# Four graph layers on one core: where the tables are turned, and who makes the distances in the sort

## The chip, the cores and the metric

The kernel runs on one core of a Trainium2 chip. The metric is the device time of one execution in microseconds, the median of several runs. The core has five engines with instruction streams of their own: TensorE (PE, with its weight loads as PEld), VectorE (DVE), ScalarE (ACT), GpSimd (POOL) and SyncE (SP, which here only issues transfers and waits). Transfers go through 16 DMA engines. Engines wait for one another with semaphores.

## The reference

There are 6250 nodes of 128 features and 200000 edges (src, dst), each with a type of 2, a type of 64 and a weight. Four graph layers follow one another, each as `x = layernorm(x + layer(x))`:

```python
x = _layernorm(x + _L0_gnn_ref(x, edge_index, edge_type_64, ...), axis=-1)      # mean of (x[src] + rel[type]) @ W_msg.T
x = _layernorm(x + _L1_gnn_ref(x, src, dst, edge_weight, ...), axis=-1)         # 4 heads, softmax over the edges of a source, norm per head
x = _layernorm(x + _L2_gnn_ref(x, edge_index, edge_type_2, ...), axis=-1)       # sum over edges, weights by type, relu
x = _layernorm(x + _L3_gnn_ref(x, edge_index, L3_gnn_W, L3_gnn_b), axis=-1)     # degree-normed sum over edges in the other direction
```

## The kernel before

The nodes are laid out in 49 tiles of 128 (NT = 49). The edges are first sorted into the 49 x 49 pairs of tiles. For each pair a one-hot product on TensorE gives a 128 x 128 table of edge counts, and every layer multiplies tables by node features. The program runs in stages, each a block that starts only when all engines have left the one before.

The sort (lines 300 to 830) works on 226 units in two phases: 49 of level 1, then 177 of levels 2 and 3 in turn. A unit holds 32 columns (level 1) or 28 (levels 2 and 3) of 128 records. For unit n, VectorE makes one-hot digits (`hot`), TensorE counts them (`count`, some 9 to 16 matmuls), ScalarE takes the counts out of PSUM (`looked`), VectorE sums them to `rank` (`ranks`), and ScalarE writes the ranks twice side by side as `place` (`paired`). Then a permutation matrix `PM` is needed for each column: 1 where the place equals the index. VectorE makes most columns by comparison with `iota_b` (`equal`). The last SHARE columns (6, 5, 4 for levels 1, 2, 3) are ScalarE's: `distances` (line 474) squares `rank - index`, one ACTIVATE with a bias for each column, and `near` (line 484) turns the squares into 1 or 0 with Relu(1 - square). TensorE's `route` (line 628) moves the records with one matmul per column, 32 or 28 of them, and waits for both VectorE's and ScalarE's columns. ScalarE takes the result out (`evict`). Order on TensorE in iteration n: `count(n+2)`, then now and then the linear part of the first layer (lines 651 to 658), then `route(n)`. Order on ScalarE: `paired(n)`, `distances(n)`, `evict(n-1)`, copies of the linear part, `double(n+3)`, `near(n)`, `looked(n+2)`.

The first layer (`aggregate_relation_turned`) makes 343 groups of seven tables each ([128, 7 x 128] in bf16, 224 KB), and SP stores each to DRAM as `tab_d` (line 1188). The second layer (`aggregate_weighted`, block at line 1612) makes its own weighted tables on TensorE, ScalarE and VectorE and moves nothing: its SP program loads one vector and is then done. The third layer (`aggregate_typed_turned`) reads the stored groups back with plain transfers (line 1931) into a ring of five buffers. The fourth (`aggregate_plain_turned`) needs each table turned. Its SP issues for each of the 343 units one `dma_start_transpose` (line 2336) that gathers seven tables from DRAM and writes them turned into a ring of five buffers (`kept`, in `sl_f`). A buffer is issued again once the conversion that read it is done. Conversion from bf16 to fp32r (line 2322) goes to `tables_r`, two buffers: even units on VectorE, odd units on ScalarE, and a conversion waits for the matmuls of the unit two before. TensorE then does four matmuls (line 2454). After each 49 units the sums are taken out by ScalarE (`sumT`, line 2428), turned by TensorE (line 2464), and seven tiles of nodes are normed by VectorE and ScalarE in slots between the units.

## Time and profile before

| | us |
|---|---|
| median of 3 runs | 4126.3 (4124.19 to 4128.95) |
| profiled execution | 4132.2, its span 4130.5 |
| TensorE busy | 3511.6 (85%) |
| VectorE busy | 3204.4 (78%) |
| ScalarE busy | 2337.2 (57%) |
| mean granted TensorE clock | 0.963 |
| chain that ended last | 10% DMA `sl_f<-tables`, in the fourth layer |

The span falls into the sort (from the start to about 1000 us), the first layer (to about 1788), the second (1788.7 to 2815.9), the third (to 3641) and the fourth (3645 to the end). A share of busy time over the whole span says little: each stage has a limit of its own, and a block ends when its last engine is done. The views used below are the windows (busy time by engine in a stretch), the lines of one instruction (durations, times to landing), the waits and the timeline.

### The profile page before, as it was taken

To read this page: it belongs to the slowest core of one execution; us is meant where nothing else is said; L and a number is where in the kernel's file an instruction comes from. 1 tells how busy PE (TensorE), PEld (TensorE's weight loads), DVE (VectorE), ACT (ScalarE), POOL (GpSimd) and SP (SyncE) were. 2 spreads that over 40 slices of the span, in tenths; PEclk is the share of its full clock that TensorE was granted. 3 is DMA by queue.
4 is the path that set the end of the run, shared out by engine and by line. 5 is a ranking of instruction groups with operands and counts; after the bars stand their busy time and mean duration, and the time that the engine had idled before them with its cause. 6 is when DMAs were issued, how large, how long until landed. Compare 5 with 4: busy or idle time off the path is not lost. (4 is left out here: it accounts for less than half of the span.)

```text
span 4130.5 us, 90438 instructions
## 1 busy us (share of the span) xinstructions
PE 3511.6 (85%) x36615; PEld 2901.3 (70%) x36740; DVE 3204.4 (78%) x3960; ACT 2337.2 (57%) x5142; POOL 391.8 (9%) x336
## 2 busy tenths in 40 slices
PE   2666777776999999869999999996999999967776
PEld 1555666664666666569999999995888888845554
DVE  7999999998777777589999999996666666723233
ACT  4998999996555555423333333334666666634343
POOL 3003211122111111100000000001000000000000
PEclk9999999997999999879999999998999999989999
DMA  3000000001322222200000000002333333268988
GB/s 107 2 2 2 2 2 2 2 2 37 114 110 110 111 111 110 77 2 2 2 2 2 2 2 2 2 2 85 99 101 101 99 101 103 86 116 170 168 170 172
DMA packets 423099, 257.10 MB, mean 62 GB/s; under 512 B 329994, under 2 KB 419863, under 8 KB 422548
## 3 DMA queue, kind: packets, MB, share of 16 engines
q1 hardware_dynamic: 422196, 248.79, 22.7%
q8 instruction: 299, 4.90, 0.5%
q10 hardware_dynamic: 480, 2.40, 0.2%
q14 instruction: 124, 1.02, 0.1%
HBM read 86.93 MB, written 85.49 MB: 42 GB/s over the span
## 5 line engine op out<-in xcount | busy, mean ns | idle before, releaser
L97 DVE TENSOR_TENSOR both_hot<-iota_own,recs 128x1792 bf16<-128x1792 bf16 (+1 forms) x686 | 754.4, 1107 | 231.5 <-PE rR L1466 121.9
L1830 ACT ACTIVATE gC<-qC 128x896 f32<-128x896 f32 x343 | 314.7, 918 | 647.6 <-PE qC L1850 647.6
L1862 PE MATMUL qO<-A,gC 128*128 128x132 f32 x4802 | 615.3, 280 | 0.0
L1862 PEld LDWEIGHTS qO<-A,gC 128*128 128x128 f32 x4802 | 566.6, 190 | 0.0
L1474 PE MATMUL rO<-sl_f,terms 128*128 128x384 bf16 (+1 forms) x1934 | 476.4, 355 | 3.7 <-DVE A L1242 2.2
L2174 ACT ACTIVATE some_r<-rC 128x512 fp32r<-128x512 f32 (+1 forms) x686 | 336.4, 543 | 252.6 <-PE rC L2204 252.1
L628 PE MATMUL pV<-VO,PM 128*128 128x70 bf16 (+4 forms) x6524 | 259.8, 199 | 236.2 <-ACT PM L484 159.7
L1432 ACT ACTIVATE sl_f<-rC 128x896 bf16<-128x896 f32 x343 | 313.8, 915 | 255.2 <-PE rC L1454 254.4
L2454 PE MATMUL tO<-tables_r,Xr 128*128 128x448 f32 x1372 | 357.6, 392 | 116.5 <-ACT tables_r L2322 80.1
L91 DVE TENSOR_TENSOR PM<-iota_b,place 128x2944 bf16<-128x2944 bf16 (+2 forms) x226 | 410.4, 1816 | 30.8 <-ACT place L464 30.4
L1466 PE MATMUL rR<-rel_hot,both_hot 128*128 128x65 bf16 x2450 | 410.9, 194 | 25.5 <-DVE A L1242 12.2
L628 PEld LDWEIGHTS pV<-VO,PM 128*128 128x128 bf16 x6524 | 238.6, 100 | 260.2 <-issue 258.3
L2454 PEld LDWEIGHTS tO<-tables_r,Xr 128*128 128x128 f32 x1372 | 234.7, 190 | 237.0 <-ACT tables_r L2322 145.1
L2322 DVE CAST tables_r<-sl_f 128x896 fp32r<-128x896 bf16 x172 | 107.8, 627 | 331.6 <-DMA sl_f<-tables 312.0
L1668 DVE TENSOR_TENSOR g<-sl_f 128x2688 bf16<-128x2688 bf16 (+1 forms) x229 | 363.9, 1589 | 0.2 <-PE qC L1850 0.2
L2216 PE MATMUL rK<-some_r,Xr 128*128 128x512 f32 (+1 forms) x1372 | 363.4, 386 | 0.0
L1850 PE MATMUL qC<-g,sl_f 128*128 128x128 bf16 x4908 | 313.9, 220 | 49.0 <-DVE g L1668 48.7
L2216 PE MATMUL rA<-all_r,Xr 128*128 128x512 f32 (+1 forms) x1372 | 342.0, 371 | 1.9 <-DVE all_r L1975 1.9
L474 ACT ACTIVATE apart_b<-iota_b,rank 128x128 bf16<-128x128 bf16 x1093 | 342.6, 396 | 0.0
L1474 PEld LDWEIGHTS rO<-sl_f,terms 128*128 128x128 bf16 x2058 | 202.1, 98 | 194.3 <-issue 20.3
L1850 PEld LDWEIGHTS qC<-g,sl_f 128*128 128x128 bf16 x4908 | 292.4, 98 | 58.1 <-DVE g L1668 54.7
L2322 ACT ACTIVATE tables_r<-sl_f 128x896 fp32r<-128x896 bf16 x171 | 162.6, 951 | 283.2 <-DMA sl_f<-tables 263.7
(298 smaller groups left out, 6225.4 us busy)
## 6 DMA issues: line engine op xcount, KB each, us to landing
tables<-sl_f SPq DMA_DIRECT2D x343, 224.0 KB, 1.9
sl_f<-tables SPq DMA_DIRECT2D x343, 224.0 KB, 2.5
sl_f<-tables SPq DMA_TRANSPOSE x343, 3.7
edges<-terms SPq DMA_DIRECT2D x1, 3528.0 KB, 11.2
B<-in_x SPq DMA_DIRECT2D x1, 2744.0 KB
out<-B SPq DMA_DIRECT2D x7, 392.0 KB
terms<-in_edge_type ACTq DMA_DIRECT2D x2, 686.0 KB
terms<-in_edge_weight ACTq DMA_DIRECT2D x1, 686.0 KB
```

The costliest lines, as they stand in the source:

```text
L91: return v.tensor_tensor(o.rearrange("p n (a b) -> p n a b", b=2), (iota_own if own else iota_b)[:, at:at + w].rearrange("p (a b) -> p a b ...
L97: return v.tensor_tensor(o.rearrange("p n k (a b) -> p (n k) a b", b=2), iota_own[:, 0:w].rearrange("p (a b) -> p a b", b=2).unsqueeze(1). ...
L474: ins = act.activation(apart_b[:, j, :], iota_b[:, 0:P], ACT.Square, scale=-1.0, bias=rank[:, n % 2, col:col + 1])
L628: mm = pe.matmul(pV[n % 2][:, g * row:(g + 1) * row].rearrange("p (f b) -> p f b", f=u.nf), PM[:, n % 2, col, :], values[:, :, col, :], st ...
L1466: return pe.matmul(pR[:, to:to + DW], both_hot[:, U % HOTS, j, 0, :], rel_hot[:, K % 2, a % FOUR * n + j, 0:DW], start=a == 0 and j == 0, ...
L1474: mm = pe.matmul(pO[:, h, 0:(hi - lo) * P], X[:, a, s, :], of_half(kept[U % RING], h), start=a == 0 and s == 0, stop=a == NT - 1 and s == ...
L1668: v.tensor_tensor(h1[:, U % 2, 0:n, :, :].rearrange("p n s (a b) -> p n s a b", b=2), bare[U % 3][:, 0:n, 1, :].rearrange("p n (a b) -> p ...
L1850: mm = pe.matmul(pC[U % 2][:, tile_in_group(q, j), :], bare[U % 3][:, j, 0, :], h1[:, U % 2, j, s, :], start=s == 0 and (q > 0 or j != 1), ...
L1862: mm = pe.matmul(pO[i % SUMS][:, 0:XW], Cs[:, U % 2, j, :], A[:, a, :], start=a == 0, stop=a == NT - 1)
L2174: act.activation(of_half(some_r[:, U % 2, :], h).rearrange("p (n d) -> p n d", d=P), pC[Q % 3][:, 0:hi - lo, :], ACT.Copy).then_inc(s_cs, 1)
L2216: mm = pe.matmul((pA if whole else pK)[:, h, 0:(hi - lo) * P], Xr[:, a, s * P:(s + 1) * P], of_half((all_r if whole else some_r)[:, U % 2, ...
L2454: mm = pe.matmul(pO[:, h, 0:HW], Xr[:, b, s * P:(s + 1) * P], table_h[:, h, :], start=b == 0 and s == 0, stop=b == NT - 1 and s == 1, skip ...
```

## The change

Two edits that don't touch each other.

First, the turned tables. A second DRAM tensor `turned_d` is added, and a buffer of three slots in SBUF. In the second layer, SP now issues for each unit a transposing transfer from `tab_d` into a slot, waits for it two units later, and stores the slot to `turned_d`. Before a slot is used again its store must have landed. The fourth layer then reads `turned_d` with plain transfers. The waits of the third and fourth layers on `s_tab` count the additional transfers.

Second, the sort. The distances `place - index` are made by TensorE: for groups of four columns, one matmul with an identity over the broadcast places and one with minus the identity over the index, summed in PSUM (`pZ`). ScalarE squares all of them with one ACTIVATE. SHARE for level 3 goes from 4 to 5. `looked(n+1)` now stands behind `paired(n)`, and `distances(n)` behind `evict(n-1)`. On TensorE `apart_from(n)` stands at the head of iteration n, between `route(n-1)` and `count(n+2)`. GpSimd makes two more constants, and VectorE and TensorE wait for 14 constants where they waited for 12.

```diff
-            SHARE = (6, 5, 4)
+            SHARE = (6, 5, 5)
...
+                    gp.tensor_scalar(whole_b[:, :], ident_f[:, :], 1.0, None, ALU.mult).then_inc(consts, 1)
+                    gp.tensor_scalar(minus_b[:, :], ident_f[:, :], -1.0, None, ALU.mult).then_inc(consts, 1)
+                    gp.wait_ge(consts, 14)
...
+                        act.wait_ge(s_far, n + 1)
                         if n >= 1:
                             act.wait_ge(s_rest_perm, n)
-                        for j in range(share):
-                            col = cols - share + j
-                            ins = act.activation(apart_b[:, j, :], iota_b[:, 0:P], ACT.Square, scale=-1.0, bias=rank[:, n % 2, col:col + 1])
-                        ins.then_inc(s_pair, 1)
+                        act.activation(apart_b[:, 0:share, :], pZ[:, 0:share, :], ACT.Square).then_inc(s_pair, 1)
...
                             paired(n)
-                            distances(n)
+                            if n > a and n + 1 < b:
+                                looked(n + 1)
                             if n > a:
                                 evict(n - 1)
+                            distances(n)
...
                             near(n)
-                            if n + 2 < b:
-                                looked(n + 2)
...
+                    def apart_from(n):
+
+                        u = units[n]
+                        cols, share = u.npos * u.ngrp, SHARE[u.level - 1]
+                        pe.wait_ge(s_pair, 2 * n + 1)
+                        for a in range(0, share, 4):
+                            w = min(4, share - a)
+                            held = place[:, n % 2, cols - share + a:cols - share + a + w, 0:1].broadcast_to([P, w, P])
+                            pe.matmul(pZ[:, a:a + w, :], whole_b[:, :], held, start=True, stop=False, skip_group_check=True)
+                            mm = pe.matmul(pZ[:, a:a + w, :], minus_b[:, :], iota_b[:, 0:P].unsqueeze(1).broadcast_to([P, w, P]), start=False, stop=True, skip_group_check=True)
+                        mm.then_inc(s_far, 1)
...
                         for n in range(a, b):
+                            apart_from(n)
                             if n + 2 < b:
                                 count(n + 2)
```

```diff
+        TURNS = 3
+        TURNED = [STORED[b] + (32 * len(range(b, UNITS, TURNS)) if b < TURNS else 0) for b in range(RING)]
...
+                        for U in range(UNITS + TURNS - 1):
+                            if U < UNITS:
+                                m, b = U // NT, U % NT
+                                first = b // G7 * NT + m * G7
+                                if U >= TURNS:
+                                    sp.wait_ge(s_tab[U % TURNS], STORED[U % TURNS] + 32 * (U // TURNS))
+                                sp.dma_start_transpose(turning[:, U % TURNS, :], tab_d[first:first + G7, :, b % G7 * P:(b % G7 + 1) * P].rearrange("u p d -> (u p) d")).then_inc(s_tab[U % TURNS], 16)
+                            done = U - (TURNS - 1)
+                            if done >= 0:
+                                sp.wait_ge(s_tab[done % TURNS], STORED[done % TURNS] + 32 * (done // TURNS) + 16)
+                                sp.dma_start(turned_d[done], turning[:, done % TURNS, :]).then_inc(s_tab[done % TURNS], 16)
+                        for b in range(TURNS):
+                            sp.wait_ge(s_tab[b], TURNED[b])
...
-                            m, b = unit(U)
-                            first = b // G7 * NT + m * G7
-                            table = tab_d[first:first + G7, :, b % G7 * P:(b % G7 + 1) * P].rearrange("u p d -> (u p) d")
-                            sp.dma_start_transpose(kept[U % RING], table).then_inc(s_tab[U % RING], 16)
+                            sp.dma_start(kept[U % RING], turned_d[U]).then_inc(s_tab[U % RING], 16)
```

## Rows read from the trace of the kernel before

**Rows 1.** Windows: second, third, fourth layer; length, PE, PEld, DVE, ACT, POOL, clock, DMA share.

```profile
1788.70:2815.90 1027.20, 980.26 (x12152) 966.80 (x12152) 991.37 (x950) 356.68 (x429) 96.19 (x99) 0.99 0.01 2
2815.90:3641.00 825.10, 798.49 (x5716) 665.00 (x5716) 557.52 (x805) 532.38 (x998) 0.00 (x0) 0.98 0.33 97
3645.07:4114.90 469.83, 360.64 (x1413) 239.85 (x1414) 139.57 (x286) 184.92 (x225) 0.00 (x0) 0.99 0.90 169
```

**Rows 2.** Waits of SP: us in total, times, longest; the second layer's block end.

```profile
SPq L1612 <- PEq L1612: 1027.2, 1, 1027.2
```

**Rows 3.** Line 2336, transposing transfers: ns to issue; first one alone, then all.

```profile
L2336 SPq DMA_TRANSPOSE sl_f<-tables x1: 1261/1261/1261, 3645.1 to 3645.1; - x1
...
DMA to landing us min/median/max: 3.5/3.5/3.5
...
L2336 SPq DMA_TRANSPOSE sl_f<-tables x343: 1150/1287/2780, 3645.1 to 4110.1; - x172
```

**Rows 4.** Line 1188, plain stores of the first layer: ns to issue, us to landing.

```profile
L1188 SPq DMA_DIRECT2D tables<-sl_f x343: 332/332/357, 1005.9 to 1717.6; - x172
...
DMA to landing us min/median/max: 1.9/1.9/4.5
```

**Rows 5.** Windows behind the first transposing issue: last columns clock, DMA share, GB/s.

```profile
3646.25:3646.50 0.25, 0.00 (x0) 0.00 (x0) 0.00 (x0) 0.00 (x0) 0.00 (x0) 0.50 0.11 27
...
3647.50:3647.75 0.25, 0.00 (x0) 0.00 (x0) 0.00 (x0) 0.00 (x0) 0.00 (x0) 0.50 0.50 103
```

**Rows 6.** A plain store's issue (timeline) and its last window of traffic.

```profile
1301.14 0.33 SPq L1188 DMA_DIRECT2D tables<-sl_f  x1
...
1302.50:1302.75 0.25, 0.25 (x6) 0.13 (x3) 0.00 (x0) 0.25 (x2) 0.00 (x0) 1.00 0.26 86
```

**Rows 7.** Timeline of the fourth layer where buffers were full: start, length, what.

```profile
3721.88 0.95 ACT L2322 ACTIVATE tables_r<-sl_f 128x896 fp32r<-128x896 bf16 x1 [2.19 <-PE tO L2454]
...
3724.06 0.95 ACT L2322 ACTIVATE tables_r<-sl_f 128x896 fp32r<-128x896 bf16 x1 [1.23 <-PE tO L2454]
```

**Rows 8.** Waits in the fourth layer: TensorE for the sums being taken out.

```profile
PE tO L2454 <- ACT sumT L2428: 7.7, 6, 1.6
```

**Rows 9.** Line 723, the ranks, one for each unit of the sort.

```profile
L723 DVE TENSOR_REDUCE rank<-M x226: 259/558/695, 67.7 to 979.0; 128x28 f32<-128x392 bf16 x47, 128x28 f32<-128x448 bf16 x37, 128x32 f32<-128x448 bf16 x25, 128x28 f32<-128x112 bf16 x4
```

**Rows 10.** Timeline of the sort, level 1: near, route, count, double, the next route.

```profile
181.72 0.92 ACT L484 ACTIVATE PM<-apart_b,ones_f 128x768 bf16<-128x768 bf16 x1
...
182.89 1.44 PE L628 MATMUL pV<-VO,PM 128*128 128x84 bf16 x32 [1.61 <-ACT PM L484]
...
184.17 0.35 PE L607 MATMUL pR<-O,tri_b 128*128 128x448 bf16 x1
...
185.35 0.56 ACT L435 ACTIVATE V<-terms 128x448 bf16<-128x448 bf16 x1
...
186.99 1.44 PE L628 MATMUL pV<-VO,PM 128*128 128x84 bf16 x32 [1.61 <-ACT PM L484]
```

**Rows 11.** Timeline of the sort, level 2: two routes in a row.

```profile
280.18 1.08 PE L628 MATMUL pV<-VO,PM 128*128 128x70 bf16 x28 [1.96 <-ACT PM L484]
...
283.57 1.08 PE L628 MATMUL pV<-VO,PM 128*128 128x70 bf16 x28 [0.87 <-ACT PM L484]
```

**Rows 12.** Groups: ScalarE's distances; then ScalarE reading PSUM, 312 and 896 elements.

```profile
L474 ACT ACTIVATE apart_b<-iota_b,rank 128x128 bf16<-128x128 bf16 x1093 | 342.6, 396 | 0.0
...
L493 ACT ACTIVATE terms<-pV 128x312 bf16<-128x312 f32 x38 | 16.1, 423 | 2.7 <-PE pV L628 2.7
...
L1432 ACT ACTIVATE sl_f<-rC 128x896 bf16<-128x896 f32 x343 | 313.8, 915 | 255.2 <-PE rC L1454 254.4
```

**Rows 13.** Groups by shape, 315 to 975 us: VectorE's comparisons, 24 and 23 columns.

```profile
L91 DVE TENSOR_TENSOR PM<-iota_b,place 128x3072 bf16<-128x3072 bf16 x85 | 153.0, 1801 | 8.7 <-ACT place L464 8.7
L91 DVE TENSOR_TENSOR PM<-iota_b,place 128x2944 bf16<-128x2944 bf16 x83 | 144.2, 1737 | 19.4 <-ACT place L464 19.1
```

**Rows 14.** Timeline at the sort's start: GpSimd's last constant, which VectorE waits for.

```profile
63.47 0.55 POOL L373 TENSOR_SCALAR lift<-ident_f 128x128 bf16<-128x128 f32 x1
```

More of the change, by code:

```diff
@@ L68, in gnn_four_layers_kernel @@
     tab_d = nc.dram_tensor("tables", (UNITS, P, G7 * P), BF16, kind="Internal").ap()
+    turned_d = nc.dram_tensor("turned_tables", (UNITS, P, G7 * P), BF16, kind="Internal").ap()
     with ExitStack() as ctx:
@@ L170, in gnn_four_layers_kernel @@
             lift = sb("lift", [P, P], BF16, c1)
+            whole_b = sb("whole_b", [P, P], BF16, c1)
+            minus_b = sb("minus_b", [P, P], BF16, c1)
             drop = sb("drop", [P, 1], F32, c1)
@@ L198, in gnn_four_layers_kernel @@
             pV = [ps(f"pV{i}", [P, 512], c1) for i in range(2)]
-            pD = ps("pD", [P, 512], c1)
+            pZ = ps("pZ", [P, 8, P], c1)
             pL = ps("pL", [P, 2, P], c1)
             pW = ps("pW", [P, 512], c1)
+            pD = pW
             names = ("loads", "pads", "consts", "tri_made", "prep", "fields", "blanks", "packed", "s_pad0", "s_load0", "s_xin0", "s_stored", "turned", "wt_made",
-                     "s_dup", "s_hot", "s_cnt", "s_look", "s_taken0", "s_more", "s_pair", "s_val", "s_perm", "s_rest_perm", "s_out", "s_ev",
+                     "s_dup", "s_hot", "s_cnt", "s_look", "s_taken0", "s_more", "s_pair", "s_val", "s_perm", "s_rest_perm", "s_far", "s_out", "s_ev",
                      "s_tp0", "s_xt0", "s_y0", "s_own0", "s_high0", "s_rest0", "s_mid0", "s_low0", "s_wt0", "s_total", "s_words", "s_named", "s_kind", "s_left", "s_last")
             (loads, pads, consts, tri_made, prep, fields, blanks, packed, s_pad, s_load, s_xin, s_stored, turned, wt_made,
-             s_dup, s_hot, s_cnt, s_look, s_taken, s_more, s_pair, s_val, s_perm, s_rest_perm, s_out, s_ev,
+             s_dup, s_hot, s_cnt, s_look, s_taken, s_more, s_pair, s_val, s_perm, s_rest_perm, s_far, s_out, s_ev,
              s_tp, s_xt, s_y, s_own, s_high, s_rest, s_mid, s_low, s_wt, s_total, s_words, s_named, s_kind, s_left, s_last) = [sem(n, c1) for n in names]
@@ L373, in _ @@
                     gp.tensor_scalar(lift[:, :], ident_f[:, :], LIFT, None, ALU.mult).then_inc(consts, 1)
-                    gp.wait_ge(consts, 12)
+                    gp.tensor_scalar(whole_b[:, :], ident_f[:, :], 1.0, None, ALU.mult).then_inc(consts, 1)
+                    gp.tensor_scalar(minus_b[:, :], ident_f[:, :], -1.0, None, ALU.mult).then_inc(consts, 1)
+                    gp.wait_ge(consts, 14)
                     def low_parts(m):
@@ L630, in route @@
                         mm.then_inc(s_out, 1)
-                    pe.wait_ge(consts, 12)
+                    pe.wait_ge(consts, 14)
                     for a, b in phases:
@@ L702, in _ @@
                     v.wait_ge(prep, PREP)
-                    v.wait_ge(consts, 12)
+                    v.wait_ge(consts, 14)
                     def hot(n):
@@ L1592, in aggregate_weighted @@
                 Cs = sb("gC1", [P, 2, G7, P], F32, c)
+                turning = sb("turning1", [P, TURNS, G7 * P], BF16, c)
                 vec = sb("vec1", [P, P], F32, c)
@@ L1973, in convert @@
                                 v.wait_ge(s_all, U - 1)
-                            v.wait_ge(s_tab[U % RING], STORED[U % RING] + 16 * (U // RING + 1))
+                            v.wait_ge(s_tab[U % RING], TURNED[U % RING] + 16 * (U // RING + 1))
                             v.tensor_copy(all_r[:, U % 2, :], kept[U % RING]).then_inc(s_kept[0], 1)
@@ L2119, in convert @@
                                 act.wait_ge(s_all, U - 1)
-                            act.wait_ge(s_tab[U % RING], STORED[U % RING] + 16 * (U // RING + 1))
+                            act.wait_ge(s_tab[U % RING], TURNED[U % RING] + 16 * (U // RING + 1))
                             act.activation(all_r[:, U % 2, :], kept[U % RING], ACT.Copy).then_inc(s_kept[1], 1)
@@ L2312, in fetched @@
                 def fetched(U):
-                    return 2 * STORED[U % RING] + 16 * (U // RING + 1)
+                    return TURNED[U % RING] + STORED[U % RING] + 16 * (U // RING + 1)
                 def converted(eng, U):
```

## The prediction

> **What bounds the kernel now.** I read the windows by stage first, then who waits inside each stage the change touches, then the timeline there. In the second layer TensorE is busy 980 of 1027 us and VectorE 991, and the DMA engines stand idle at a share of 0.01 [rows 1]. SP has nothing to do there: it waits 1027.2 us for the block to end [rows 2]. In the fourth layer no engine is full (TensorE 361 of 470 us), but the DMA share is 0.90 [rows 1]. Each of its 343 units costs SP a transposing issue of 1.29 us, and the first one, with nothing in flight, already took 1.26 [rows 3]. 343 x (1.29 + 0.03 to the next) is 453 of the 470 us, so the fourth layer goes by SP's issuing. In the sort two engines are level: the level-1 period is 4.10 us from route to route (182.89 to 186.99) [rows 10], which is VectorE's four operations back to back, and ScalarE's list is just as long. The whole span's 57% for ScalarE hides that.
>
> **The fourth layer, where work is removed.** The transposing issue (1.29 us) becomes a plain one (0.33 us for a plain transfer of the same 224 KB) [rows 3, 4]. The ring of five then no longer sets the pace: the third layer drew 97 GB/s at a DMA share of 0.33 [rows 1], so a unit costs 0.33 x 825 / 343 = 0.79 us of the DMA engines. Late next is the pair of buffers `tables_r`: an odd unit's conversion (ScalarE, 0.95 us), its four matmuls, then the next odd conversion. The trace shows this loop bare where the ring was full: conversions start at 3721.88 and 3724.06 [rows 7], 2.18 us for two units, 1.09 for one. 343 x 1.09 = 374. To it comes a first landing of about 3 us, and six changes of tile group, which can no longer hide behind the ring: TensorE waits 7.7 / 6 = 1.3 us for the sums [rows 8], turns seven tiles (I put 0.9), and VectorE's three wide additions overfill its slots (I put 1.7): an estimate of 3.9 us, 24 for six. 374 + 3 + 24 = 401 against 470: minus 69. Bounds: minus 95 if nothing of the 24 shows, minus 55 if it is half as much again.
>
> **The second layer, where SP gets work.** This is the largest term. 343 transposing issues and 343 stores go on SP's queue, in one order. Iteration U is: wait for the store of U-3, issue transpose U, wait for transpose U-2, issue store U-2. But the store of U-3 was issued in iteration U-1, right before. Three slots do not help: every iteration contains a whole store from issue to landing. The wait for transpose U-2 costs nothing, it was issued two iterations earlier.
>
> The room is 1027.2 / 343 = 2.99 us per unit [rows 2]. The need, from below: 1.31 us until the store can be issued (1.29 and the step to it), 1.9 us until it has landed, the shortest and the median of 343 stores alone [rows 3, 4], 0.04 to go on: 3.25 us. From above: the store goes on the same queue right behind a transpose whose data has barely begun. The transpose issued at 3645.07 has its traffic from about 3646.4 (0.11 in that window, its issue just over) to the dip at 3647.6 [rows 5], so 1.3 to 2.6 us after its issue. A store issued at 1301.14 has sent its last bytes at about 1302.6, in a burst of 0.6 to 0.7 us [rows 6], and lands 0.4 us after. Behind the transpose the burst lies at 2.6 to 3.25, and the landing at 3.7: 3.75 with the step. I take 3.6, near the upper end, because the DMA engines are full with the transpose when the store's data would begin at 2.05; I leave something for the ragged start and end of its traffic.
>
> The end: 342 iterations and the last transpose and store one behind the other (3.5 + 1.9). 1788.7 + 342 x 3.6 + 5.4 = 3025, where the block now ends at 2815.9: plus 209. At 3.25 it is plus 90, at 3.75 plus 261. All engines wait for SP there, and the third layer cannot start. That the DMA engines are idle in this layer is true and no cover: a chain of latencies is what has to fit, not a transfer rate.
>
> A rule points the same way. The Trainium skill ("DMA: Bandwidth & Descriptors", section "Queues, rings and completion order") says that a ring is consumed in order and that a semaphore's increment lands only after all earlier writes of that DMA engine. By it a store's landing cannot come before the transpose's own, 3.5 us after its issue, so the lower bound of 3.25 would be 3.55. No row here shows a plain transfer behind a transpose, so I keep 3.25 as a bound.
>
> **The sort.** At the start GpSimd makes two more constants like `lift`, 0.55 us each [rows 14], and VectorE and TensorE wait for them: plus 1. Removed are ScalarE's 6, 5 or 4 activations, 342.6 / 1093 = 0.31 us each; added is one reading PSUM: from 0.42 us for 312 elements and 0.92 for 896, 0.81 for 768 and 0.70 for 640 [rows 12]. ScalarE gains 1 us per unit, yet VectorE is as full as it was in level 1. VectorE gains only 1.80 - 1.74 us for 86 units of level 3 (5 us) and the waits for `place`, 8.7 + 19.1 us [rows 13]: at most minus 33.
>
> Against that, the new wait closes a loop that did not exist: `route(n)`, then on the same queue `apart_from(n+1)`, then ScalarE's square, `double`, `near`, and `route(n+1)`, which needs `near`. Before, ScalarE made its distances while TensorE routed. Queued behind the wait for `s_far` on ScalarE are `double` and `near`; TensorE waits for these. Level 1, from the rows: `near` ends at 182.64 and route starts at 182.89, 0.25; route to the next matmul 1.28 (182.89 to 184.17) [rows 10]; 2 x 768 columns at 2.4 GHz 0.64; tail of the last matmul 0.16 (0.35 less the 0.19 of 448 columns); to ScalarE 0.1; square 0.81 - 0.1; double 0.56 - 0.1; near 0.92 [rows 10, 12] (0.1 is what neighbours on ScalarE overlap). Sum 4.52 against 4.10: 48 periods x 0.42 = plus 20. Level 2: route 1.08 instead of 1.44, 640 columns, the rest a little shorter, some 3.76 against 3.39 (280.18 to 283.57) [rows 11]. But the mean of the second phase is well above 3.39: from 67.7 to 979.0 us there are 225 periods [rows 9], less 48 x 4.10, so 177 of 4.04. Its extra work (the linear part, words, clock at its lower level) may cover the longer loop or add to it. I take plus 0.08 each, plus 15; bounds minus 33 and plus 62 (0.35 each). Sort: plus 36, from minus 12 (1 + 20 - 33) to plus 83; minus 32 if the loop of level 1 is not closed either.
>
> **Sum.** 209 - 69 + 36 = plus 176. The profiled span of 4130.5 would be 4307; the median of the runs lies 4 us below that span, so 4126.3 + 176 = 4302.
>
> **Rivals.** A: the forecast, SP's chain of about 3.6 us; 4302, its own range 4215 to 4390.
>
> B: the store is not held up by the transpose in front, 3.25 us. For it: the stores landed in 1.9 us while anything else was going on. Against: those had an empty queue. 4126 + 90 - 69 + 36 = 4183.
>
> C, the other side: SP's chain fits under TensorE and VectorE, so the second layer keeps its 1027 us. Mechanism: the 1.26 us issue is not SP's own work but the queue pushing back, and in a queue that is drained every iteration it falls to a plain issue's 0.33 [rows 4], so an iteration is 2.3 us. It decides from 3.09 us down, where (1027.2 + 33 - 5.4) / 342 the added end eats the gain. For it: 1.29 is nearly the pace of the fourth layer. Against: the very first issue, nothing in front, took 1.26 [rows 3]. 4126 - 69 + 36 = 4093, or 4025 if the sort gives its 33 as well. The Trainium skill ("Advanced Engine Details and Errata", section "X-Bar Transpose (TRN2)") says that transposing transfers are as fast as regular ones, which would be this rival; the trace has 169 GB/s in the fourth layer [rows 1] against some 350 in a plain store's burst (224 KB in 0.65 us [rows 6]), so I don't follow it.
>
> D: reading `tab_d` and writing `turned_d` at once makes both slower, 4.2 us: plus 415, 4508.
>
> That the edit in the sort does not relieve ScalarE is not a rival: five activations of 0.31 become one of 0.7. Whether that relief reaches the end is the question above.
>
> **Chances.** A 0.62, B 0.17, C 0.12, D 0.09. The range 4125 to 4420 takes in A and B and leaves out most of C, D. About 0.2% (8 us) is what a measurement of this kernel can tell from no change. Faster: most of C and a thin end of B with the sort's best case, 0.12. Same: 0.03. Slower: 0.85.
>
> **What would show it.** In the changed kernel, SP's wait for the end of the block in the second layer is gone and the others wait for SP, some 200 us; DMA there shows a period of 3.6 us, with stores landing in about 2.3 instead of 1.9. The fourth layer's conversions wait for matmuls, 2.18 us apart, and DMA leaves the chain that ended last. In the sort, TensorE's idle time before `route` is given to `near`, and level 1 runs at 4.5 us per unit. I am wrong if the second layer still ends with TensorE's last matmul, or if the level-1 period stays at 4.10.

## The result, and the profile after

The changed kernel takes 4363.06 us (median, 4361.89 to 4379.83) against 4127.62 for the kernel before on the same chip: a ratio of 1.0582 (1.0561 to 1.0602), 235 us slower. The profiled execution has a span of 4360.2 us against 4130.5, so 229.7 us have to be found. SP's waits in the second layer (us in total, times, longest):

```profile
SPq L1642 <- DMA turned_tables<-turning: 693.9, 340, 4.1
SPq L1646 <- DMA turning<-tables: 0.9, 1, 0.9
```

In place of the one wait of 1027.2 us for the others [rows 2] SP now waits 340 times for a store to land, and only once for a transpose. The ends of the block, line 1632, say who was late:

```profile
L1632 PEldq DRAIN  x1: 2188/2188/2188, 2797.3 to 2797.3; - x1
...
L1632 DVEq DRAIN  x1: 911/911/911, 2821.6 to 2821.6; - x1
...
L1632 SPq COMPARE_BRANCH  x1: 41/41/41, 3126.6 to 3126.6; - x1
```

The other engines are done at 2822.5, 1027.9 us after the layer began at 1794.6, which is their old time. SP follows 304 us later. Its issues there (ns to issue, shortest/median/longest, first and last; below each line the us from issue to landing):

```profile
L1642 SPq DMA_TRANSPOSE turning<-tables x343: 1151/1152/2172, 1795.0 to 3121.5; - x172
...
DMA to landing us min/median/max: 2.9/3.1/5.1
...
L1646 SPq DMA_DIRECT2D turned_tables<-turning x343: 320/578/1044, 1799.1 to 3124.7; - x172
...
DMA to landing us min/median/max: 1.9/2.4/4.7
```

(3121.5 - 1795.0) / 342 is 3.88 us for one iteration. But it is not the same all along. The timeline of SP in the tail, where all others stand, and windows beside one another (columns as in [rows 1]):

```profile
2999.09 1.15 SPq L1642 DMA_TRANSPOSE turning<-tables  x1
3000.29 0.58 SPq L1646 DMA_DIRECT2D turned_tables<-turning  x1
3002.68 1.15 SPq L1642 DMA_TRANSPOSE turning<-tables  x1
```

```profile
1900.00:2000.00 100.00, 96.69 (x1194) 94.82 (x1192) 97.11 (x101) 32.55 (x37) 7.25 (x10) 1.00 0.46 114
2850.00:2950.00 100.00, 0.00 (x0) 0.00 (x0) 0.00 (x0) 0.00 (x0) 0.00 (x0) 0.50 0.48 125
```

In the tail an iteration takes 3.59 here and 3.61 on average (83 iterations from 2821.8 to 3121.5); while the engines run, 259 issues in 1026.8 us make 3.96. The traffic says the same: 114 against 125 GB/s.

The fourth layer, in the timeline at its end and over all (the matmuls of line 2484):

```profile
4099.95 0.95 ACT L2355 ACTIVATE tables_r<-sl_f 128x896 fp32r<-128x896 bf16 x1 [1.24 <-PE tO L2484]
4100.96 1.88 PE L2484 MATMUL tO<-tables_r,Xr 128*128 128x448 f32 x8 [0.28 <-ACT tables_r L2355]
4102.13 0.95 ACT L2355 ACTIVATE tables_r<-sl_f 128x896 fp32r<-128x896 bf16 x1 [1.23 <-PE tO L2484]
```

```profile
L2484 PE MATMUL tO<-tables_r,Xr x1372: 358/367/742, 3959.4 to 4344.8; 128*128 128x448 f32 x196
```

ScalarE's conversions stand 2.18 us apart. Of the 343 conversions 311 wait for matmuls now, where it was 21 before: the loop over the two buffers sets the pace all along, and not only where the ring happened to be full [rows 7]. From the first transfer's issue, 3956.2, to the last matmul, 4344.8, it is 388.6 us against 469.8: minus 81. Of the chain that ended last, transfers are 0% now where they were 10%.

The sort, level 1 in the timeline, then all ranks:

```profile
179.30 0.81 ACT L479 ACTIVATE apart_b<-pZ 128x768 bf16<-128x768 f32 x1 [0.22 <-PE pZ L628]
180.47 0.93 ACT L488 ACTIVATE PM<-apart_b,ones_f 128x768 bf16<-128x768 bf16 x1
181.66 1.45 PE L644 MATMUL pV<-VO,PM 128*128 128x84 bf16 x32 [1.34 <-ACT PM L488]
182.94 0.38 PE L627 MATMUL pZ<-place,whole_b 128*128 128x512 bf16 x1
183.14 0.43 ACT L497 ACTIVATE terms<-pV 128x312 bf16<-128x312 f32 x1 [1.07 <-PE pV L644]
183.79 0.81 ACT L479 ACTIVATE apart_b<-pZ 128x768 bf16<-128x768 f32 x1 [0.22 <-PE pZ L628]
```

```profile
L740 DVE TENSOR_REDUCE rank<-M x226: 258/558/619, 68.7 to 992.5; 128x28 f32<-128x392 bf16 x47, 128x28 f32<-128x448 bf16 x37, 128x32 f32<-128x448 bf16 x25, 128x28 f32<-128x112 bf16 x4
```

Square to square is 4.49 us (and 4.53 in some periods), against 4.10 [rows 10], and TensorE waits for `PM`, ScalarE for `pZ` and `pV`, in a closed ring. The last rank comes at 992.5 instead of 979.0 [rows 9].

The ledger: up to the last rank +13.5; from there to the second layer -7.6 (802.1 instead of 809.7); the second layer +305.1 (1332.3 instead of 1027.2); from its end to the fourth's first issue +0.1; the fourth layer -81.2; behind it -0.2. Together 229.7.

### The profile page after: what moved, and what is told of

Read it like the earlier page. It is cut to its first block and busy times, and to the rows that moved or that the text cites. A ratio compares the mean times of both kernels' runs of the same rounds, so it can differ in the third digit from the quotient of the medians.

```text
span 4360.2 us, 92418 instructions
## 1 busy us (share of the span) xinstructions
PE 3580.6 (82%) x37643; PEld 2962.3 (68%) x37644; DVE 3207.1 (74%) x3960; ACT 2206.9 (51%) x4275; POOL 389.8 (9%) x338
## 5 line engine op out<-in xcount | busy, mean ns | idle before, releaser
L1493 PE MATMUL rO<-sl_f,terms 128*128 128x512 bf16 (+1 forms) x2058 | 500.3, 354 | 19.7 <-DVE A L1261 13.0
L2237 PE MATMUL rC<-both_hot 128*128 128x128 bf16 x2450 | 197.3, 221 | 336.3 <-DVE both_hot L98 336.3
L92 DVE TENSOR_TENSOR PM<-iota_b,place 128x2944 bf16<-128x2944 bf16 (+1 forms) x226 | 407.4, 1803 | 14.3 <-ACT place L470 13.9
L2237 PEld LDWEIGHTS rC<-both_hot 128*128 128x128 bf16 x2450 | 138.4, 98 | 392.5 <-DVE both_hot L98 341.5
L2008 DVE CAST all_r<-sl_f 128x896 fp32r<-128x896 bf16 x172 | 107.6, 626 | 397.9 <-DMA sl_f<-tables 311.4
L2484 PE MATMUL tO<-tables_r,Xr 128*128 128x448 f32 x1372 | 329.4, 382 | 64.0 <-ACT tables_r L2355 42.5
L2484 PEld LDWEIGHTS tO<-tables_r,Xr 128*128 128x128 f32 x1372 | 245.3, 189 | 145.9 <-ACT tables_r L2355 104.6
```

Source lines behind the costliest of these rows:

```text
L92: return v.tensor_tensor(o.rearrange("p n (a b) -> p n a b", b=2), (iota_own if own else iota_b)[:, at:at + w].rearrange("p (a b) -> p a b ...
L1493: mm = pe.matmul(pO[:, h, 0:(hi - lo) * P], X[:, a, s, :], of_half(kept[U % RING], h), start=a == 0 and s == 0, stop=a == NT - 1 and s == ...
L2237: mm = pe.matmul(pC[Q % 3][:, to - lo, :], both_hot[:, U % HOTS, j, 1, :], both_hot[:, U % HOTS, j, 0, :], start=m > 0 or j != 1, stop=m > ...
L2484: mm = pe.matmul(pO[:, h, 0:HW], Xr[:, b, s * P:(s + 1) * P], table_h[:, h, :], start=b == 0 and s == 0, stop=b == NT - 1 and s == 1, skip ...
```

## The experiments

**Is it the turned tables, and those alone?** The change in halves: `e3_turn_only` has the sort of the kernel before, `e4_sort_only` the second to fourth layers of the kernel before.

> The kernel before with the edit of the tables alone, the sort as before. Theory: all of the loss is here: plus 305 in the second layer, minus 81 in the fourth, about 4351, some 14 us under the changed kernel. Rival (the new sort costs nothing of its own, its 14 us are the clock's): 4363.

> The kernel before with the edit of the sort alone. Theory: level 1 is 0.42 us per unit longer (plus 20), the second phase a little shorter (minus 8), plus 1 for the constants: plus 13 in the sort, 4127 + 13 = 4140, less what the first layer gains in clock (8 us in the profile of the changed kernel). Rival (ScalarE's relief shows): below 4120.

Measured: the tables alone 4352.11 (4347.4 to 4355.6), ratio 1.0546 (1.053 to 1.0562); the sort alone 4142.42 (4141.12 to 4147.87), ratio 1.004 (1.0026 to 1.0054). Neither half is a gain, and the two add up: 223 + 14 against 235.

**Is it that the store stands behind the transpose on the queue?** `e1_store_first` issues in each iteration the same two transfers in the other order, the store of U-2 ahead of transpose U. `e2_four_slots` leaves the order and gives the store one slot more, so that the one waited for was issued an iteration earlier.

```diff
                        for U in range(UNITS + TURNS - 1):
+                            done = U - (TURNS - 1)
+                            if done >= 0:
+                                sp.wait_ge(s_tab[done % TURNS], ...)
+                                sp.dma_start(turned_d[done], turning[:, done % TURNS, :])...
                             if U < UNITS:
                                 ...
                                 sp.dma_start_transpose(turning[:, U % TURNS, :], ...)...
-                            done = U - (TURNS - 1)
-                            if done >= 0:
-                                ...
```

```diff
-        TURNS = 3
+        TURNS = 4
-                        for U in range(UNITS + TURNS - 1):
+                        for U in range(UNITS + TURNS - 2):
-                            done = U - (TURNS - 1)
+                            done = U - (TURNS - 2)
```

> The changed kernel with one edit on SP in the second layer: in each iteration the store of unit U-2 is issued before the transposing transfer of unit U, not behind it. The same 686 transfers, the same three slots. Theory (the period is a chain: issue of the transpose, then a whole store from issue to landing, because the store waited for was issued in the iteration just before): the landing now runs under the next transpose's issue, the period falls from 3.9 us to about 2 us, 343 x 2 = 690 us fits under the 1027 us of TensorE and VectorE, and the second layer ends at its old length. Time 4363 - 305 = about 4058. Rival (the DMA engines or the mix of reading and writing DRAM set the 3.9 us, whatever the order): the period stays above 3.5 us and the time above 4300.

> The changed kernel with four slots instead of three, and the store still two units behind the transpose and issued after it: the store waited for is now one iteration older. Theory of the chain: two iterations hold one transpose issue, one store landing and another transpose issue, so the period falls to 2 to 2.4 us and the second layer is back at about 1027 us, the time at about 4060. If only the order on the queue mattered (a store behind a transpose is slow), the period would stay above 3.5 us.

Measured: 4062.5 (4057.04 to 4067.5), ratio 0.9841 (0.9826 to 0.9856); and 4066.7 in a single run. The same two transfers in another order are worth 300 us. SP is now done before the others (ns to issue, landing, then the layer's windows):

```profile
L1646 SPq DMA_TRANSPOSE turning<-tables x343: 1149/1200/2773, 1799.9 to 2599.4; - x172
...
DMA to landing us min/median/max: 3.0/3.2/5.8
```

```profile
2000.00:2200.00 200.00, 196.70 (x2449) 194.32 (x2449) 195.00 (x184) 73.61 (x91) 18.15 (x20) 1.00 0.92 197
```

An iteration is (2599.4 - 1799.9) / 342 = 2.34 us, far less than 3.61, and under the 2.99 that the layer allows. The DMA engines are at 0.92 with 197 GB/s while TensorE is busy 196.70 of 200 us, as it was with next to no traffic beside it (196.69 in the same window of the kernel before, at a share of 0.01): in this layer the transfers don't slow the computing. The second layer was lost to latencies in a row, not to a rate.

**Is it the transposing transfer, or any transfer in front of the store?** `e5_plain_in` replaces the transpose by a plain load of the same size; it leaves out the turning, and reads one stored group where the transpose gathers seven tables.

```diff
-                                sp.dma_start_transpose(turning[:, U % TURNS, :], tab_d[...])...
+                                sp.dma_start(turning[:, U % TURNS, :], tab_d[U])...
```

> The changed kernel with the transposing transfer of the second layer replaced by a plain load of the same 224 KB (the tables stay unturned, so the fourth layer sums over the wrong side); order, slots and waits as in the changed kernel. Theory of the chain: an iteration is the issue of the load (0.33 us) and a whole store, 0.33 + 2.4 + 0.1 = 2.8 to 3.2 us with the disturbances of the busy part, so the second layer is near or little over its 1027 us, the time 4060 to 4110. Rival (the traffic of reading and writing at once sets the 3.9 us): it stays above 4300.

Measured: 4186.89 in a single run, 77 us over the upper end of what was expected. An iteration is (2950.3 - 1804.2) / 342 = 3.35 us, although the issue in front of the store is short:

```profile
L1642 SPq DMA_DIRECT2D turning<-tables x343: 319/320/431, 1804.2 to 2950.3; - x172
...
DMA to landing us min/median/max: 2.4/2.7/4.3
...
L1646 SPq DMA_DIRECT2D turned_tables<-turning x343: 319/432/1671, 1808.2 to 2953.0; - x172
...
DMA to landing us min/median/max: 1.9/2.9/4.6
```

The store, issued 0.4 us behind the load, lands 2.9 us after its issue, where one with nothing in front lands in 1.9 [rows 4]. Both kernels say the same: the store lands 0.5 to 0.6 us after the transfer ahead of it has landed. Plain: 0.4 + 2.9 = 3.3 against 2.7. Transposing, in the quiet tail: issued 1.2 after the transpose and landing in 2.4 is 3.6, against 3.1. That is the forecast's upper picture, and it doesn't need the transpose. The Trainium skill ("DMA: Bandwidth & Descriptors", section "Queues, rings and completion order") has a ring consumed in order and the increment after earlier writes; these traces agree, with 0.5 to 0.6 us on top. They don't separate the order of the queue from the 16 DMA engines that both transfers share: no run issues the store from another queue.

**Why 3.96 us while the engines run, and 3.61 when they stand?** In the timeline some iterations are 1 to 2 us longer. One of them, with the windows of traffic in it (last columns DMA share and GB/s):

```profile
1806.71 0.58 SPq L1646 DMA_DIRECT2D turned_tables<-turning  x1
1811.18 1.15 SPq L1642 DMA_TRANSPOSE turning<-tables  x1
```

```profile
1808.50:1809.00 0.50, 0.50 (x10) 0.48 (x9) 0.50 (x1) 0.00 (x0) 0.00 (x0) 1.00 0.00 0
1809.00:1809.50 0.50, 0.50 (x12) 0.50 (x10) 0.50 (x1) 0.00 (x0) 0.00 (x0) 1.00 0.05 5
1809.50:1810.00 0.50, 0.50 (x11) 0.50 (x8) 0.31 (x1) 0.01 (x1) 0.00 (x0) 1.00 0.07 11
1810.00:1810.50 0.50, 0.50 (x6) 0.50 (x6) 0.44 (x1) 0.50 (x1) 0.00 (x0) 1.00 0.81 307
```

For 1.5 us next to nothing moves; then the rest comes. The view of the DMA queues has, beside the queue of the data, two that bring instructions. First from 1795 to 2822 us, then in the tail (packets, MB, share of 16 engines):

```profile
q8 instruction: 96, 1.57, 0.7%
q14 instruction: 25, 0.20, 0.1%
```

```profile
q14 instruction: 1, 0.01, 0.0%
```

Counted by iteration between 1800 and 2820 us, a packet belonging to the iteration in which it begins: the 146 in which neither queue has a packet take 3.62 us on average, and none is over 4.2. (The text put on record before the next run has 154 of them, with the same average, and 3.57 for the tail.) The 96 with a packet of q8 take 4.53, and 54 of them are over 4.2; the 13 with one of q14 alone take 4.02. The 3.62 is the tail's 3.61: TensorE and VectorE at work beside the transfers cost them nothing that shows. In `e1_store_first` it is 2.05 for the 248 without and 3.27 for the 76 with one of q8. To tell the fetching from the mere activity of the engines, `e12_tail_work` puts useless work into the quiet tail: first many small matmuls (many instructions, little data), then wide operations on VectorE and ScalarE (few instructions, much data in SBUF and PSUM).

```diff
+                        pe.wait_ge(s_cs, UN)
+                        for r in range(2000):
+                            mm = pe.matmul(pC[0][:, 0, 0:32], bare[0][:, 0, 0, :], h1[:, 0, 0, 0, 0:32], start=True, stop=True, skip_group_check=True)
+                        mm.then_inc(s_c, 1)
...
+                        act.wait_ge(s_c, UN + 1)
+                        for r in range(130):
+                            act.activation(Cs[:, 0, :, :], pC[0][:, 0:G7, :], ACT.Copy).then_inc(s_cs, 1)
+                            act.wait_ge(s_cs, UN + r + 1)
...
+                        v.wait_ge(s_c, UN + 1)
+                        for r in range(80):
+                            v.tensor_tensor(h1[:, 0, 0:n, :, :]..., ALU.mult).then_inc(s_hot, 1)
+                            v.wait_ge(s_hot, UN + r + 1)
```

> The changed kernel with useless work put behind the second layer's real work, while SP goes on turning tables alone. First 2000 small matmuls on TensorE (4000 instructions with their weight loads, 32 columns, in some 126 us), then, when they are done, 80 wide multiplications on VectorE (some 1.55 us each) and 130 copies out of PSUM on ScalarE (0.92 us), 210 instructions in about 125 us. Open is why SP's iteration takes 3.96 us while the engines run and 3.57 when they stand. In the changed kernel's trace, between 1800 and 2820 us, 154 iterations without any packet of the two instruction queues take 3.62 us on average and none over 4.2; 96 with a packet of the larger instruction queue take 4.53. Theory (the fetching of instructions holds the transfers up): a packet brings some 256 instructions, so the stretch of small matmuls has about 16 packets, each costs 0.9 us, and its iterations take about 4.0 us on average (16 x 0.9 / 34 = 0.42 over 3.57); the stretch of wide operations stays at 3.6. Rival (SBUF and PSUM traffic of busy engines holds the transfers up): the stretch of wide operations has 3.9 and more, that of small matmuls 3.6 to 3.7. If the fetching theory holds, the kernel takes 4363 + 14 = 4377, else 4363 + 15 or more if the wide operations cost their 0.4 on 33 iterations, so only the stretches tell them apart. A window of traffic in a long iteration should show an instruction packet where the transfers stand still.

Measured: the matmuls kept TensorE busy for 52 us, not 126 (26 ns each). SP's transposes in that stretch, 2799 to 2852 us, and its packets; then the stretch of wide operations, 2856 to 2976:

```profile
L1642 SPq DMA_TRANSPOSE turning<-tables x13: 1151/1236/2196, 2800.2 to 2848.6; - x13
```

```profile
q8 instruction: 15, 0.25, 1.9%
```

```profile
L1642 SPq DMA_TRANSPOSE turning<-tables x33: 1151/1152/1659, 2855.8 to 2972.5; - x33
```

```profile
q8 instruction: 1, 0.02, 0.0%
```

From 2800.17 to the issue at 2852.16 it is 13 iterations of 4.00 us; those from 2823.90, with TensorE alone at work, began with 5.51, 4.35 and 4.04. From 2860.04 to 2972.49 it is 31 of 3.63; the quiet rest is 3.60. TensorE itself, too, stops for 0.1 to 0.7 us after every 128 weight loads and 128 matmuls, and 4000 instructions over 15 packets are about as many for each packet (timeline):

```profile
2818.25 3.27 PEld L1916 LDWEIGHTS qC<-g,sl_f 128*128 128x128 bf16 x128 [0.48 <-issue]
...
2822.00 3.27 PEld L1916 LDWEIGHTS qC<-g,sl_f 128*128 128x128 bf16 x128 [0.48 <-issue]
```

So wide operations cost 0.03 and the stretch with the packets 0.40: of the two rivals the fetching stands. That it isn't TensorE's own work follows from the 146 iterations above and from four here, at 2837.8 to 2848.6, which took 3.59 like any other. The size was off: 15 packets on 13 iterations cost 5.2 us, 0.35 each and not 0.9. The time of 4359.26 us, a single run, is 18 under the 4377 expected; at this size it tells nothing.

Those four iterations have a packet each, so a packet alone doesn't decide. What a packet costs depends on when it begins, counted from the iteration's transposing issue. In the changed kernel the 23 iterations with a packet in the first 1.3 us take 4.11 us on average. The 38 in which it begins 2.25 to 3.0 us in, while both transfers are under way, take 5.27, and none is under 4.84; the long one shown above is of these, with its packet at 2.76. The 19 in which it begins 3.1 to 3.5 us in, when the transpose has just landed, take 3.72, with one at 5.24 and all others at most 3.89. `e3_turn_only` has 5.24 for 39 and 3.80 for 29 in the same two groups. The four of `e12_tail_work` lie at 3.07 to 3.25. By what path a packet stops the other transfers is open.

**Is the pair of buffers what is late next in the fourth layer?** `e6_three_buffers` is e1 with three buffers `tables_r`.

```diff
-                tables_r = sb("tables_r3", [P, 2, G7, P], F32R, c)
+                tables_r = sb("tables_r3", [P, 3, G7, P], F32R, c)
-                    if U >= 2:
-                        eng.wait_ge(s_o, U - 1)
+                    if U >= 3:
+                        eng.wait_ge(s_o, U - 2)
```

> The changed kernel with the store issued first (as in the run of that name) and with three buffers of converted tables in the fourth layer instead of two. Theory (in the changed kernel's fourth layer the 2.18 us for two units are ScalarE's conversion of 0.95 us and four matmuls of 1.09 us in series on one buffer): the pair is now bound by TensorE's eight matmuls, 1.9 us, so 343 units lose 0.14 us each, 48 us; about 4062 - 48 = 4014. Rival (TensorE or the transfers are already the bound): no change, 4060.

Measured: 4000.38 (3993.43 to 4002.48), ratio 0.9685 (0.9669 to 0.9701). The matmuls go from 3662.1 to 3982.4, 320 us where e1 has 385.5 (3659.7 to 4045.2): the loop over the buffer was the limit, and a little more hung on it than I had put, 62 us in the median and not 48.

**Where does the sort lose its time?** By the forecast mostly in level 1, in the loop route, distances, square, near. `e7_level1_old` (with e1) lets ScalarE make level 1's distances again from `rank`, but in the new order, behind `evict`. `e9_level1_whole` gives level 1 the old order too, distances ahead of `evict`. `e11_order_only` is the kernel before with nothing but ScalarE's new order. `e8_all` is e7 with the three buffers.

```diff
                     def distances(n):
                         ...
+                        if u.level == 1:
+                            for j in range(share):
+                                ins = act.activation(apart_b[:, j, :], iota_b[:, 0:P], ACT.Square, scale=-1.0, bias=rank[...])
+                            ins.then_inc(s_pair, 1)
+                            return
...
                             paired(n)
+                            if units[n].level == 1:
+                                distances(n)
                             if n > a and n + 1 < b:
                                 looked(n + 1)
                             if n > a:
                                 evict(n - 1)
-                            distances(n)
+                            if units[n].level > 1:
+                                distances(n)
...
-                            apart_from(n)
+                            if units[n].level > 1:
+                                apart_from(n)
```

This is e9; e7 has all of it but the second part. And e11, on the kernel before:

```diff
                             paired(n)
-                            distances(n)
+                            if n > a and n + 1 < b:
+                                looked(n + 1)
                             if n > a:
                                 evict(n - 1)
+                            distances(n)
...
                             near(n)
-                            if n + 2 < b:
-                                looked(n + 2)
```

> The changed kernel with the store issued first, and with level 1 of the sort making its distances as before (one activation per column on ScalarE, nothing on TensorE), levels 2 and 3 as changed. Theory (the loop route, apart_from, square, double, near, route closes at 4.52 us in level 1): the level-1 period returns to 4.10 us, minus 20: 4062 - 20 = 4042. Rival (the longer period comes from the new place of looked and distances in ScalarE's order, which stays): 4062.

> The three edits together on the changed kernel: store first in the second layer, three converted buffers in the fourth, level 1 of the sort as before. If the three are independent, 4062 - 48 - 20 = 3994.

> As the run of level 1 made the old way, but with ScalarE's order of level 1 also as before: distances in front of evict(n-1), levels 2 and 3 as changed, store first in the second layer. Theory after that run: there are two loops through ScalarE, not one. With evict in front of distances, a route must end before distances start: 0.25 + 1.44 + 0.1 + evict 0.33 + six squares 1.75 + double 0.46 + near 0.92 = 5.25 us, as the run showed; with both restored, the level-1 period is 4.10 us and the time 4062 - 20 = 4042. Rival (the changed kernel's 4.5 us come from something else, say the place of looked): above 4055.

> The kernel before with ScalarE's new order in the sort alone (looked(n+1) behind paired(n), distances behind evict(n-1)); the distances are made on ScalarE as before. Theory of the evict loop: level 1 at 5.1 to 5.3 us per unit instead of 4.10 (plus 50), the second phase at 0.25 + 1.08 + 0.1 + 0.25 + 1.5 + 0.4 + 0.8 = 4.4 us and more where it had 4.0 (plus 70 to 110), more still where TensorE's clock falls: 4250 to 4300. Rival (the order is harmless and level 1 made the old way was slow for another reason): 4120 to 4135.

Measured: e7 4130.88 (4125.39 to 4132.64), ratio 1.0006 (0.9996 to 1.0015), 89 us over what I expected; e8 4067.37 (4064.85 to 4070.81), ratio 0.9852, 73 over; e9 4050.93 (4049.01 to 4051.75), ratio 0.9819 (0.9803 to 0.9836); e11 4251.69 in a single run, 127 us slower than the kernel before. That total is what I expected, but by luck in part: from the first rank to the 49th it is 5.66 us per unit and not 5.1 to 5.3, plus 75 where I had 50, and the second phase has 4.33 and not 4.4 and more, plus 52 where I had 70 to 110. The timeline of e7, in two places:

```profile
106.39 1.45 PE L650 MATMUL pV<-VO,PM 128*128 128x84 bf16 x32 [1.82 <-ACT PM L494]
...
111.63 2.40 PE L650 MATMUL pV<-VO,PM 128*128 128x84 bf16 x32 [1.75 <-ACT PM L494]
...
180.26 2.40 PE L650 MATMUL pV<-VO,PM 128*128 128x84 bf16 x32 [1.70 <-ACT PM L494]
182.70 0.43 ACT L503 ACTIVATE terms<-pV 128x312 bf16<-128x312 f32 x1 [2.03 <-PE pV L650]
183.02 1.85 ACT L481 ACTIVATE apart_b<-iota_b,rank 128x128 bf16<-128x128 bf16 x6
185.24 0.92 ACT L494 ACTIVATE PM<-apart_b,ones_f 128x768 bf16<-128x768 bf16 x1
186.42 2.40 PE L650 MATMUL pV<-VO,PM 128*128 128x84 bf16 x32 [1.71 <-ACT PM L494]
```

What failed in my expectation for e7 is that the period returns to 4.10 as soon as TensorE doesn't make the distances: behind `evict` they begin only when the route has ended, and with six activations (1.85 us) in place of one (0.81) the loop is longer than that of the change. With the route at 1.45 us a unit takes some 5.2 us (5.24 at 106.39, and e9's text works it out as 5.25). On top of it TensorE, which now has the same work in a longer period, is granted its lower level (1.2 GHz) for part of the time; 32 matmuls of the route take 2.40 us there, inside the loop, and the unit 6.16. Level 1 in windows, e7 and then e9:

```profile
66.00:245.00 179.00, 114.26 (x1262) 87.67 (x1261) 131.94 (x127) 129.11 (x343) 0.00 (x0) 0.75 0.10 29
```

```profile
66.00:245.00 179.00, 109.50 (x1751) 89.76 (x1749) 176.84 (x174) 176.41 (x476) 0.00 (x0) 1.00 0.11 31
```

In e9, ScalarE and VectorE are full again (176 of 179), the granted clock is 1.00, and the period 4.10. The last rank comes at 979.8 us, where e1 has 994.4: 14.6 us, which is most of what level 1 was to have cost. In the median it is 11.6. From e7 to e9 only the place of level 1's distances changes, and it is worth 80 us.

**A version that beats both.** `e10_best` is e9 with the three buffers: tables turned in the second layer with the store ahead of the transpose, TensorE's distances for levels 2 and 3 alone.

> The same with three converted buffers in the fourth layer. If level 1's 20 us come back, 4000 - 20 = 3980; if not, 4000.

Measured: 3983.46 (3981.33 to 3987.72), ratio 0.9653 (0.9637 to 0.967), 142 us under the kernel before. Nothing shows that TensorE's distances have a part in it: the last rank comes at 981.3 us here and at 979.8 in e9, and with the sort left as it was at 979.0 (the kernel before) and 974.4 (e3). The gain is in the second and fourth layers; both edits there on the untouched sort were not run.

## Why the prediction was right, and where it was off

The forecast was slower by 176 us, by SP's chain. It was slower, by SP's chain, by 235.

**Second layer, +209 forecast, +305 measured.** The mechanism was right: each iteration holds a store from issue to landing, behind a transpose. The term of the sum that was mis-sized is the 3.6 us. The trace has it at 3.61 where the queue is by itself. Over the layer it is 3.88: 342 x 0.28 = 96 us, all of the miss. The rows that I took my latencies from were single ones; the mean of an iteration has the fetching of instructions in it: the 96 iterations with a packet of q8 are 0.91 us longer than those without one, 87 of the 96 us. That 3.6 met 3.61 in the quiet tail is in part luck. The upper picture of 3.75 had the store's landing right (2.39 us from its issue) and put that issue at 1.31 us, where it comes at 1.20: the transposing issue in front takes 1.15 and not 1.29, a figure that had the fourth layer's full queue in it [rows 3]. What I took off for the ragged start and end of the traffic was not there.

**The rivals.** B (the store is not held up, 3.25) falls: the store lands in 2.4 us and not in 1.9, and in e5 it waits even behind a plain load. C (the 1.26 us was a queue pushing back) falls: with nothing in flight the issue still takes 1.15. D (reading and writing together are slower, 4.2 us) falls: the quiet iteration is 3.61, and with both at 197 GB/s in e1 a transpose lands in 3.2. C's end, on the other side, is reached by another way, the order of two issues: e1's 4062 lies between C's 4025 and 4093.

**Fourth layer, -69 forecast, -81 measured.** The 2.18 us for two units is exact. The 24 us that I put for six changes of tile group were too much: 388.6 - 374 - 3 leaves 12. (The lower bound of the forecast, with nothing of the 24, comes to minus 93 and not 95.)

**The sort, +36 forecast, +13.5 measured.** Constants +1 (first rank 68.7 instead of 67.7) and level 1's period of 4.52 (measured 4.49 and 4.53) are right; from the first rank to the 49th it is 17 us more, and e9 takes level 1 back and gains 14.6. The term that failed is the second phase, +15 forecast, -5 measured (710.1 us from the 49th rank to the last instead of 714.9). The longer loop is there: where it is bare, routes of level 2 stand 3.71 us apart (forecast 3.76) and not 3.39 [rows 11].

```profile
301.01 1.08 PE L644 MATMUL pV<-VO,PM 128*128 128x70 bf16 x28 [0.65 <-ACT PM L488]
304.72 1.08 PE L644 MATMUL pV<-VO,PM 128*128 128x70 bf16 x28 [0.64 <-ACT PM L488]
```

What I had wrong is to add it to the mean. The short periods got longer and the long ones shorter: the quartiles of the periods are 3.50 and 4.36 us before, 3.70 and 4.00 after. VectorE's waits for `place` fall from 30.4 to 13.9 us between 275 and 975 us, and TensorE, with the distances as new work, is busier at a higher clock (before, then after):

```profile
275.00:975.00 700.00, 529.37 (x7887) 425.85 (x7884) 663.91 (x906) 632.05 (x2087) 149.37 (x113) 0.94 0.01 2
```

```profile
275.00:975.00 700.00, 596.41 (x8573) 464.43 (x8573) 662.31 (x899) 545.64 (x1458) 146.49 (x113) 0.98 0.01 2
```

Which of these did it, no run separates. Nor are the 5 us a gain of the edit: the same phase takes 711.1 us in e3, with the old sort, and 715.3 in e9, with the new one. It is nothing, where I had put +15.

**First layer, 0 forecast, -8 measured.** No edit touches it, and the sort is not the cause either. From the last rank to the second layer it is 809.7 us before and 802.1 after. But e2 and e5, which are the changed kernel up to that point, have 810, and e12 has 805; with the old sort, e3 has 807. The 8 us are within what executions of the same instructions differ by. From 1100 to 1700 us TensorE's granted clock is 0.99 before and 1.00 after, but 0.99 in e2 and e5 too.

## What to carry to other kernels

A copy loop on one queue is priced by what its waits enclose: write down, for each wait, how long ago the awaited transfer was issued and what stood in front of it. A store issued behind a load on the same queue landed after that load in every case here, so issue the store first, or wait for one that is an iteration older; here this was worth 300 of 4363 us, and an idle DMA and an idle issuer said nothing about it. When an edit moves work within an engine's list, look for the loop that the new place closes: made on ScalarE, the distances of level 1 alone cost 80 us more behind `evict` than ahead of it (e7, e9).

## What the runs showed of the hardware

- A transposing issue of 224 KB holds SP for 1.15 us (median) with nothing in flight, a plain load 0.32 (e5). From issue to landing they are closer: 3.1 us against 2.7.
- A store lands 0.5 to 0.6 us after the transfer in front of it on the queue has landed, be it a transpose (changed kernel) or a plain load (e5).
- DMA engines at a share of 0.92 and 197 GB/s left the computing of the layer as it was (TensorE busy 196.70 of 200 us in e1, 196.69 before).
- The fetching of instructions shows in the transfers of data: an iteration with a packet of the larger instruction queue took 4.53 instead of 3.62 us (3.27 instead of 2.05 in e1). What a packet costs depends on when it comes: 5.27 us if it begins 2.25 to 3.0 us into the iteration, 3.72 if 3.1 to 3.5. The Trainium skill ("Runtime: NRT & Kernel Launch", section "Instruction fetch mechanics") has blocks of 256 instructions, 16 KiB each, fetched ahead and mostly hidden. The size agrees with 1.57 MB in 96 packets. Hidden it is mostly for the engine that runs them (0.1 to 0.7 us of TensorE's time at each 256 small instructions in e12), not for the transfers beside them.
- TensorE's granted clock can fall in a loop that TensorE is part of, and the loop gets longer by it. In level 1 a unit of 4.10 us (e9), or of 4.49 with the distances as added work (the changed kernel), kept 1.00; in one of 5.2 us with e9's work (e7) the clock went between its two levels, 0.75 on average, the route took 1.45 or 2.40 us, and the unit up to 6.16.
